# Attention on one core: value products in two halves of the queries between the pairs of scores, and unread products in a wait of the first unit

## What is computed

```python
scores = jnp.einsum('bkgsd,bktd->bkgst', qh, kh) / scale      # G = 4 heads share a key head
weights = jax.nn.softmax(scores, axis=-1)
out = jnp.einsum('bkgst,bktd->bkgsd', weights, vh)
...
x = x + _L0_xattn_ref(...)
x = x + _L0_ffn_ref(...)
x = x + _L1_xattn_ref(_layernorm(x, axis=-1), ctx_512, ctx_512)
x = x + _L1_ffn_ref(...)                                      # top-2 routed experts
```

## Time and profile before

| | us |
|---|---|
| median of the runs shown (1652.31 to 1658.4) | 1655.52 |
| profiled execution, its own time | 1656.3 |
| its span | 1654.5 |
| attention phase in it, about 500 to 903 | 403 |
| TensorE busy in the span | 1568.1 (95%) |
| VectorE | 948.3 (57%) |
| ScalarE | 715.5 (43%) |
| GpSimd | 700.7 (42%) |

### The profile page before, as it was taken

The page is one execution under the profiler, slowest core; times in us unless marked ns, Lnnn a source line. Parts: engine busy times, 40 slices in busy tenths (PEclk is TensorE's granted clock), DMA queues, the critical chain, the costliest instruction groups (busy, mean ns, idle before and its releaser), DMA issues.

```text
span 1654.5 us, 24666 instructions
## 1 busy us (share of the span) xinstructions
PE 1568.1 (95%) x8251; PEld 1051.2 (64%) x8278; DVE 948.3 (57%) x1540; ACT 715.5 (43%) x1166; POOL 700.7 (42%) x479
## 2 busy tenths in 40 slices
PE   6879999999989999999998899999999999999998
PEld 3565657565754333434333778888888888888886
DVE  6998979797888898888885522222222222222221
ACT  5885645555546777767676211111111111111111
POOL 1224261534523126254464765670872170930074
PEclk9889999999999999999999899999999999999999
DMA  9189800000231445343430634323520323410088
GB/s 356 66 305 386 296 1 1 1 1 1 83 96 36 122 138 148 91 128 118 145 115 28 226 109 149 132 76 131 186 77 26 140 76 127 154 62 26 26 144 212
DMA packets 90946, 196.18 MB, mean 119 GB/s; under 512 B 7154, under 2 KB 9075, under 8 KB 90227
## 3 DMA queue, kind: packets, MB, share of 16 engines
q1 hardware_dynamic: 71746, 156.68, 28.2%
q0 software_dynamic: 7168, 17.04, 4.5%
q10 hardware_dynamic: 11952, 21.43, 3.9%
HBM read 113.28 MB, written 81.32 MB: 118 GB/s over the span
## 4 chain that ended last, share of the span: by engine, by line
PE 75%; DVE 15%; ACT 3%; issue 3%; POOL 2%; DMA 1%; another core or an unknown queue 0%; SPq 0%; DVEq 0%; POOLq 0%; ACTq 0%
PE psum L2970 13%; PE psum L2972 13%; PE psum L2971 13%; PE psum L2613 7%; PE psum L2824 6%; PE psum L2813 5%; DVE neg_max L2088 4%; PE psum L2658 3%; PE psum L2787 3%; PE psum L2993 2%; PE psum L2628 2%; DVE inner_rotated_t_second L1952 1%; DMA x_tiles<-in_x 1%; DVE inner_t L1947 1%; DVE inner_t L1946 1%
## 5 line engine op out<-in xcount | busy, mean ns | idle before, releaser
L2088 DVE TENSOR_REDUCE neg_max<-psum 128x2 f32<-128x1024 f32 x248 | 292.0, 1220 | 43.1 <-PE psum L2787 40.8
L1447 ACT ACTIVATE probabilities<-psum 128x512 f32<-128x512 f32 x512 | 269.8, 604 | 82.3 <-PE psum L2813 77.7
L2230 DVE TENSOR_TENSOR expert_inner<-psum,expert_inner 128x512 f32<-128x512 f32 x78 | 54.0, 692 | 384.6 <-ACT expert_inner L1552 384.6
L2970 PE MATMUL psum<-expert_weight_parts,sorted_tokens_t_first 128*128 x624 | 251.0, 402 | 3.9 <-issue 2.1
L2972 PE MATMUL psum<-expert_weight_parts,sorted_tokens_t_second 128*128 x624 | 247.7, 397 | 0.0
L2971 PE MATMUL psum<-expert_weight_parts,sorted_tokens_t_first 128*128 x624 | 247.7, 397 | 0.0
L1552 ACT ACTIVATE expert_inner<-psum 128x512 f32<-128x512 f32 x78 | 46.7, 598 | 392.4 <-PE psum L2972 392.4
L2813 PE MATMUL psum<-query_rows,key_rows 50*128 50x512 f32 x512 | 182.8, 449 | 5.9 <-ACT probabilities L1447 2.2
L2787 PE MATMUL psum<-key_rows,query_rows 48*128 48x512 f32 x496 | 175.8, 482 | 7.1 <-DVE neg_max L2088 3.2
L2824 PE MATMUL psum<-probabilities,value_and_one 128*32 128x512 f32 x1024 | 139.4, 617 | 1.5 <-ACT probabilities L1447 0.9
L2970 PEld LDWEIGHTS psum<-expert_weight_parts,sorted_tokens_t_first 128*128 128x128 f32 x624 | 118.3, 190 | 31.6 <-issue 4.9
(11 more groups left out here) (317 smaller groups left out, 2974.7 us busy)
## 6 DMA issues: line engine op xcount, KB each, us to landing
sorted_x<-zero_rows SPq DMA_DIRECT2D x9, 3960.0 KB, 30.7
w_of_odd_expert<-in_L_ffn_w SPq DMA_DIRECT2D x8, 2048.0 KB
wo_of_expert<-in_L_ffn_wo SPq DMA_DIRECT2D x7, 2048.0 KB, 8.6
query_rows<-query_rows_of_units SPq DMA_DIRECT2D x64, 192.0 KB, 3.7
w_of_even_expert<-in_L_ffn_w SPq DMA_DIRECT2D x6, 2048.0 KB, 10.4
sorted_tokens<-sorted_x ACTq DMA_DIRECT2D x39, 264.0 KB, 2.7
sorted_y<-expert_out ACTq DMA_DIRECT2D x39, 256.0 KB, 2.1
query_rows_of_units<-dims_first SPq DMA_DIRECT2D x32, 256.0 KB
```

What stands on the lines that cost most here:

```text
L1447: nc.scalar.activation(prob[t % 2][:, i * SEQ:(i + 1) * SEQ], ring(("score", n)), ACT.Exp, scale=HD ** -0.5).then_inc(c_e, 1)
L2088: nc.vector.tensor_reduce(of_pair[:, p, st, :], ring(("max", (m, i))).rearrange("p (h n) -> p h n", h=2), AX.X, ALU.max, negate=True).then ...
L2230: nc.vector.tensor_tensor(h, bank[2 * half + 1], h, ALU.mult).then_inc(e_h, 1)
L2970: nc.tensor.matmul(out_bank, hi[:, cols], w_r[:, bass.ds(w_at, 512)], start=start, stop=False)
```

## The change

`attend` gets a second argument, the half of the queries. Each half is the same four matmuls with 256 columns in place of 512; the first half carries the waits, the second the signal `c_pv`. The first half is issued after the first two pairs of the next step, the second after the last two, where the whole group was. And in step 0 of unit 0, before the transposed maxima of unit 1, fourteen unread products are issued into bank 7, which holds nothing then.

```diff
--- before.py
+++ after.py
@@ -2813,20 +2813,25 @@
                 nc.tensor.matmul(ring(("score", n)), k_r[u % 4][rows, t * P:(t + 1) * P],
                                  q_r[u % 4][rows, p * SEQ:(p + 1) * SEQ], start=True, stop=True).then_inc(c_s, 1)
 
-            def attend(k):
+            def attend(k, half):
 
                 u, t = k // ST, k % ST
-                pe.wait_ge(c_e, 4 * k + 4)
-                if t == 0:
-                    pe.wait_ge(c_v, u + 1)
-                    pe.wait_ge(c_oe, u)
+                if half == 0:
+                    pe.wait_ge(c_e, 4 * k + 4)
+                    if t == 0:
+                        pe.wait_ge(c_v, u + 1)
+                        pe.wait_ge(c_oe, u)
+                queries = slice(half * SEQ // 2, (half + 1) * SEQ // 2)
                 for h in range(GROUP):
-                    last = nc.tensor.matmul(bank[7][32 * h:32 * h + 32, :], v_u[u % KVH][:, t * 32:(t + 1) * 32],
-                                            prob[t % 2][:, h * SEQ:(h + 1) * SEQ], start=(t == 0), stop=(t == ST - 1))
-                last.then_inc(c_pv, 1)
+                    of_head = prob[t % 2][:, h * SEQ:(h + 1) * SEQ]
+                    last = nc.tensor.matmul(bank[7][32 * h:32 * h + 32, queries], v_u[u % KVH][:, t * 32:(t + 1) * 32],
+                                            of_head[:, queries], start=(t == 0 and half == 0), stop=(t == ST - 1 and half == 1))
+                if half == 1:
+                    last.then_inc(c_pv, 1)
 
             def attention(u):
                 for t in range(ST):
+                    k = ST * u + t - 1
                     for p in range(2):
                         for h in range(2):
                             if there(u):
@@ -2835,10 +2840,11 @@
                                 maximum(u + 2, 2 * t + p, 1 - h, h == 0)
                         if u == -1:
                             unread(3)
-                    k = ST * u + t - 1
-                    if 0 <= k < ST * UNITS and (there(u) or t == 0):
-                        attend(k)
+                        if 0 <= k < ST * UNITS and (there(u) or t == 0):
+                            attend(k, p)
                     if t == 0 and u >= 0 and there(u + 1):
+                        if u == 0:
+                            unread(14, bank[7])
                         neg_max_transposed(u + 1)
                     if t == 1 and there(u - 1):
                         attended_transposed(u - 1)
```

## The result

| | before | changed |
|---|---|---|
| median of the runs, us | 1653.84 (1648.68 to 1658.4, 6 runs) | 1672.67 (1666.03 to 1679.08, 6 runs) |
| ratio to before, 95% interval | | 1.0122 [1.01, 1.0143] |
| profiled execution, us | 1656.3 | 1679.08 |
| its span, us | 1654.5 | 1677.0 |
| attention phase, us | 403.0 | 432.5 |

The changed kernel is 1.2% slower. The forecast was 1659 with no measurable change as the likeliest sign, and the result lies just above the upper end of its range, 1672. The attention phase runs from the first score to the first instruction behind the last unit. "Half clock" adds up the stretches in which the records of the granted clock give 0.50, that is 1.2 GHz in place of 2.4.

What follows compares the result with a forecast made beforehand. No single engine bounds the attention phase; TensorE, VectorE and ScalarE are nearly full, so step order decides. Plain units 3.7, routing units -1.5, last two +2, unread products -0.9 sum to +3.3 us: 1659 from 1655.52, range 1647 to 1672.

Steps and rivals of the forecast that it cites:

- rival 3: Attention units: the clock falls more often behind the new step 1 wait; 8 us, 1667; chance 0.08.
- A half group at 0.57: TensorE: half a value group takes 0.57 us from start to next work, bounds 0.50 and 0.68.
- The step without waits at 2.46: TensorE, one attention step without any wait: 2.46 us after the change, about 2.14 before.
- Steps 2.66, 3.69, 2.73, 2.46: Plain unit, steps 0 to 3: step 0 0.15 us shorter, step 1 0.49 longer, step 3 2.46 for 2.68.
- Fourth score at T+1.57: Step 0 of a plain unit: fourth score 1.57 us after the first, when the exponential is done; before, T+1.18.
- Wait in step 1 until T+0.65: Step 1 of a plain unit: first product for maxima waits for VectorE's reduction until T+0.65, before T+0.40.
- The unit 11.54: Whole plain unit: 11.54 us for 11.38, +0.16; over 23 units +3.7 us.
- Routing units: Units 12, 13, 20, 21, 27, 28, with routing jobs behind five of eight steps: -0.25 us each, -1.5 together.
- The last two units, +2: Last two units, without products for maxima: split scores and group take 2.02 us for 1.66 a step, +2 us.
- The unread products: Unit 0: fourteen products, 1.54 us, end inside TensorE's wait and may keep the clock at 2.4 GHz: -0.9 us.
- Rival 1: Some 124 steps: the first half fills the wait for exponentials, 21 us faster, 1634; chance 0.14.
- Rival 2: Each step: half groups at 0.68 us add 0.22 a step, 20 us in all, 1679; chance 0.12.

Runs made afterwards that it cites:

- the fills: Changed kernel plus eight unread products in step 0 of units 10, 18, 26 and 29, in waits for VectorE: 1662.69 us, 1.0062 to the kernel before.
- The kernel with step 1 filled: Changed kernel plus three unread products in step 1 of every unit, between first score and first product for maxima: 1689.12 us, ratio 1.0249.
- the kernel with both remedies: Changed kernel plus unread products ahead of transposed maxima (units 10, 18, 26, 29) and unit 30's first score, last two units' groups whole: 1661.62 us, 1.0058.

## Why the prediction was wrong

**The step that failed** is the clock. The sum of the forecast has no term for falls outside unit 0; it puts the half clock of all other units at nothing new. The prediction had the mechanism as its rival 3, saw its mark in the earlier trace rows, and priced it at "one in four loses 1.1 us as unit 0 did", 8 us, with a chance of 0.08, because "today's 0.40 in every unit doesn't do it". Both parts of that were wrong:
- *The trigger.* The new wait of 0.64 us in step 1 of every plain unit did not start the stretches: units 1 to 9 ran at the full clock. They begin behind single longer waits: 1.10 and 0.34 us in unit 10, 1.88 in unit 0 where it isn't filled, 3.50 in unit 17, 1.79 in unit 25, 0.87 and 0.34 in unit 29 and 1.29 before unit 30. Some of these the change itself made longer, which the prediction didn't look for: 1.10 us was 0.72, 0.87 was 0.67 and 1.29 was 0.95, each without a fall. In unit 10 the wait is 0.70 to 0.74 us in the four unfilled kernels without a half between the pairs of its step 0, and the clock fell there in one of them; it is 1.04 to 1.10 in the six with halves there, and the clock fell in four; where the wait is filled, in four kernels, it fell in none. So a longer wait makes a fall likelier and doesn't settle it. Counting how many units have a new wait was the wrong count.
- *The length.* The price came from a fall that ends after 3.4 us. Behind the waits of units 0 and 10 a fall lasted 3.4 us in all three cases with a whole group in step 1, and 10.2, 20.5, 23.9 and 23.9 us in the four with halves there. Over the whole phase the split is less sharp: in the six kernels with halves in all but the last two units or in all, 9 of 17 stretches lasted 10 to 24 us; in the four without a half between pairs, 2 of 10, both 10.2. A step at half clock takes 4.3 to 5.8 us (unit 10) for 2.5 to 3.7, so a stretch of 23.9 us costs 9.6 over two units (34.8 for 25.2), not 1.1. This price was in no row of the kernel before, and it wasn't bounded: a range for "how long does a fall last with the new order" was missing, and the change rewrites the order in which TensorE works.

**How much of it is shown.** That the place of the halves between the pairs causes the loss, and not their size or number, is shown (1.0122 for the change, 0.9999 with both at the end). What the fourteen unread products add to it, 1.0122 for 1.0063, is measured and not explained. That the clock carries most of the loss is shown by the steps (26.3 of the 29.5 us of the phase lie in the 14 that are slow only after) and by the fills: adding work took half the loss away. The half clock per run goes the same way: 44 to 52 us in the seven kernels with a ratio from 0.9986 to 1.001, 60 and 61 at 1.0058 and 1.0062, 71 at 1.0063, 85 at 1.0122 (the change) and at 1.013. The kernel with step 1 filled, at 86 and 1.0249, has 20 us of added work besides. *Why* a stretch lasts longer with the halves is open. TensorE has no idle time in the stretches of 20 us and more that the rows show. The wait of step 1 alone isn't it. The Trainium skill (TensorE: Matmul & The Clock Gate, A second HAM failure mode) describes a kernel whose short gaps between groups of matmuls let the clock swing between its levels. The swings are here, but the long stretches begin behind waits of about a microsecond or more, and in four of the five of the changed kernel's phase the rows show no gaps at all.

**Term by term, at the full clock.**
- A half group at 0.57: measured 0.57. The step without waits at 2.46: 2.47. Steps 2.66, 3.69, 2.73, 2.46 predicted, 2.69, 3.70, 2.73, 2.47 measured. Fourth score at T+1.57: T+1.58. Wait in step 1 until T+0.65: 0.64. The unit 11.54: 11.59, +0.21 for the +0.16 predicted, 23 times that is +4.8 for +3.7.
- Routing units (12, 13, 20, 21, 27, 28), -0.25 each: unit 13 went from 13.82 to 13.40, unit 12 from 13.41 to 13.38, unit 28 from 13.43 to 12.99. About as sized on the mean, but it falls on three of the six.
- The last two units, +2: they took 31.7 us for 20.5, nearly all of it clock. In the kernel with the halves alone they took 22.9, so +2 was right there.
- The unread products: two rows stand for each, so one takes 0.22 us and not 0.11, and fourteen 3.1 us instead of 1.54:

```profile
501.33 3.39 PE L2860 MATMUL psum<-ident 128*128 128x128 f32 x28
504.56 0.27 PE L2796 MATMUL psum<-ident,neg_max 128*16 128x128 f32 x1
```

They outlast the wait by 1.3 us (step 0 of unit 0 takes 5.04 for 3.76), and the clock stays up, so the next three steps are 2.48 each. Unit 0 is 0.7 us shorter (+1.3 in step 0, -2.0 in the other three), 0.9 was predicted: two errors that cancel, so that number came out by luck. With whole groups the products bring 0.9989 [0.9977, 1.0].
- Rival 1 (*filling wins*) got 0.14. It holds in step 3 alone, for 0.19 us a unit. Rival 2 (*dear halves*) got 0.12 and is out. The forecast's +3.3 is near what the 105 undisturbed steps gave, +4.6.

**What stays open**, beside the length of a fall: units 17 and 25 have a stall of their own. In the changed kernel VectorE has ended its last reduction by 719.92, and the products for maxima that come next have ended by 719.58 in their row. Yet it stands, and the row names no releaser on this core:

```profile
723.01 1.23 DVE L2088 TENSOR_REDUCE neg_max<-psum 128x2 f32<-128x1024 f32 x1 [3.10 <-remote]
```

and in the kernel with both remedies, where TensorE, VectorE and ScalarE each stand for more than half of 3 us while the DMA engines are 0.86 busy:

```profile
712.00:715.00 3.00, 0.89 (x10) 0.27 (x2) 1.23 (x1) 1.08 (x2) 1.94 (x3) 1.00 0.86 269
715.00:722.00 7.00, 6.97 (x39) 2.62 (x39) 5.19 (x9) 3.69 (x7) 0.90 (x2) 0.53 0.63 197
```

The kernel before has such a stall too, of 1.25 us at 711. In each of the three the half-clock stretch of unit 17 follows it. What holds the engines wasn't tried.

## What to carry to other kernels

Where a kernel keeps TensorE just busy enough, list the waits of two thirds of a microsecond and more that already stand in it, and ask how long each will be with the new order and what the clock will do behind it, not only behind the waits that the change adds; and give "how long a fall lasts" a range of its own, since it was 3.4 us in one order of the same work and 20.5 in another. One profile is one draw of these stretches: the profiles of these nearly equal programs had them in other units, so compare the mean granted clock of all runs before mending the place that one profile shows. And count the rows of a matmul kind per instruction issued before pricing it.

## What the runs showed of the hardware

- A long stretch at 1.2 GHz without any idle time of TensorE in the rows: 20.00 of 20.00 us busy at 0.50 in units 0 and 1 with the halves alone, and 20.50 of 20.50 in units 30 and 31 of the change. Being busy without a gap, as the profile counts it, did not bring the clock back.
- A wait of 1.87 us in unit 0 brought 3.4 us of half clock with whole groups behind it, one of 1.88 us brought 20.5 with halves between the pairs. In unit 10 the stretch was 3.4 us in two kernels with a whole group in step 1, and 10.2, 23.9 and 23.9 in three with halves there. Not every wait brings a fall: two kernels with 1.04 us there had none.
- Four matmuls of 256 columns side by side cost no more per column than four of 512 (both halves in a row: 1.00 us, as for the whole group; ratio 0.9999). The fixed part of a group shows only when it is cut off by other work: 0.57 against 0.50.
- An unread fp32 product of 128x128 shows as two rows and takes 0.22 us.
- VectorE stood for 3.10 us, and in another kernel for 1.99, in rows that name no releaser on this core; in both the DMA engines were 0.86 busy over the 3 us around it (720 to 723, and 712 to 715). Whether the one causes the other wasn't tried.
